# Attention tower with routed experts: down projection joined in one tail, groups of 384 rows for 512

## The reference

```python
# x: (128, 375, 512); q, k, v are its three parts of 125 rows
weight = softmax(einsum('bct,bcs->bts', q * scale, k * scale))
h = einsum('bts,bcs->bct', weight, v)
...
h = h + attn(layernorm(h))          # 8 query heads, 2 key/value heads, softcap 50
x = layernorm(h)
scores = softmax(x @ gate_w)
_, sel = top_k(scores + expert_bias, 2)
...
routed_in = xf[token_idx] * top_scores_sorted[:, None]     # sorted by expert
u = silu(ragged_dot(routed_in, w1, counts)) * ragged_dot(routed_in, w3, counts)
routed_out = ragged_dot(u, w2, counts)
out = silu(xf @ sw1) * (xf @ sw3) @ sw2                    # the shared expert
out = out.at[token_idx].add(routed_out)
h = h + out
```

## Time and profile before

| | us |
|---|---|
| three runs, median | 6056.9 |
| three runs, lowest and highest | 6055.64 and 6059.46 |
| the profiled execution | 6056.73 |
| its span, first to last instruction | 6054.8 |
| TensorE busy | 5857.1 (97%) |
| VectorE busy | 4222.9 (70%) |
| ScalarE busy | 2834.4 (47%) |
| GpSimd busy | 2044.6 (34%) |

### The profile page before, as it was taken

One profiled execution on the slowest core, in us unless ns is written; L12 is line 12 of the kernel. 1 busy time (PEld: TensorE's weight loads), 2 busy tenths in 40 slices (PEclk: granted clock), 3 DMA queues, 4 the chain that ended last, 5 costly groups with the idle time before them and its releaser, 6 DMA issues. The chain is left out here.

```text
span 6054.8 us, 103195 instructions
## 1 busy us (share of the span) xinstructions
PE 5857.1 (97%) x30728; PEld 4825.5 (80%) x30728; DVE 4222.9 (70%) x9884; ACT 2834.4 (47%) x5254; POOL 2044.6 (34%) x1725
## 2 busy tenths in 40 slices
PE   5999999999999999999999999799999999999999
PEld 4888888888888888888888887588888888888887
DVE  4777777777777777777777776566666666666665
ACT  3444444444444444444444443344444444444443
POOL 1333333333333333333333332233333333333332
PEclk8999999999999999999999999899999999999999
DMA  2111111111111111111111111566666666666641
GB/s 71 44 46 47 42 43 47 45 42 44 47 45 42 45 48 43 42 45 48 42 43 47 45 42 31 142 161 162 156 156 156 154 157 157 156 156 160 162 120 50
DMA packets 317085, 504.76 MB, mean 83 GB/s; under 512 B 78645, under 2 KB 151349, under 8 KB 316917
## 3 DMA queue, kind: packets, MB, share of 16 engines
q1 hardware_dynamic: 246132, 372.56, 20.3%
q0 software_dynamic: 70912, 131.71, 11.0%
HBM read 379.30 MB, written 140.28 MB: 86 GB/s over the span
## 5 line engine op out<-in xcount | busy, mean ns | idle before, releaser
L1402 POOL DMA_INDIRECT out_dram<-res,goal x280 | 529.2, 1890 | 1120.1 <-DMA out_dram<-res,goal 688.4
L619 ACT ACTIVATE e<-ps,shift 128x512 f32<-128x512 f32 x512 | 347.4, 683 | 672.4 <-DVE shift L718 635.3
L1146 PE MATMUL ps<-rT_hi,up_hi 128*128 128x512 f32 x1960 | 536.7, 395 | 1.6 <-DVE rT_lo L1310 1.6
L1146 PE MATMUL ps<-rT_lo,up_hi 128*128 128x512 f32 x1960 | 536.9, 395 | 0.0
L1146 PE MATMUL ps<-rT_hi,up_lo 128*128 128x512 f32 x1960 | 536.5, 395 | 0.0
L1146 PEld LDWEIGHTS ps<-rT_hi,up_hi 128*128 128x128 f32 x1960 | 369.1, 188 | 90.0 <-issue 2.0
L1146 PEld LDWEIGHTS ps<-rT_lo,up_hi 128*128 128x128 f32 x1960 | 369.1, 188 | 88.1
L1146 PEld LDWEIGHTS ps<-rT_hi,up_lo 128*128 128x128 f32 x1960 | 368.8, 188 | 88.0
L904 POOL TENSOR_SCALAR ve<-ag 125x1 f32<-125x1 f32 x256 | 57.2, 223 | 1125.2 <-DVE ag L734 1086.2
L1238 ACT ACTIVATE uT_hi<-egb 128x512 fp32r<-128x512 f32 (+1 forms) x280 | 177.1, 632 | 540.7 <-DVE egb L1329 540.5
L1233 ACT ACTIVATE eth<-ps 128x512 f32<-128x512 f32 (+1 forms) x280 | 165.5, 591 | 514.7 <-PE ps L1146 514.4
(11 more groups left out here) (210 smaller groups left out, 15235.1 us busy)
## 6 DMA issues: line engine op xcount, KB each, us to landing
raw<-in_L_ffn_w SPq DMA_DIRECT2D x140, 768.0 KB, 5.2
X<-in_x SPq DMA_DIRECT2D x128, 750.0 KB
raw<-in_L_ffn_w SPq DMA_DIRECT2D x70, 896.0 KB, 4.8
normed_rows<-y SPq DMA_DIRECT2D x128, 250.0 KB
out_dram<-h SPq DMA_DIRECT2D x128, 250.0 KB
raw<-in_L_ffn_w SPq DMA_DIRECT2D x210, 128.0 KB, 6.3
rows<-normed_rows,entries POOLq DMA_INDIRECT x280, 3.9
out_dram<-res,goal POOLq DMA_INDIRECT x280
```

The source lines that it names most:

```text
L619: nc.scalar.activation(e[:, i, :], ps[:, (i + 1) % 2, :], ACT.Exp, scale=QS, bias=shift[:, i:i + 1], accum_out=total[:, i:i + 1]).then_inc ...
L1146: ins = nc.tensor.matmul(ps[:, bank, :], w[a][:, k, col:col + P], rT[b][:, k, :], start=(k == 0 and i == 0), stop=(k == KC - 1 and i == 2))
L1402: nc.gpsimd.indirect_dma_start(out, bass.IndirectOffsetOnAxis(ap=goal[group[1] % 2][:, i:i + 1], axis=0), res[i][:], None, bounds_check=la ...
```

## The change

Three things. First, the shared expert's hidden columns are cut into three blocks of 128 and a tail of 64. The tail stands twice over the partitions, the hidden value's high part on 0 to 63 and its low part on 64 to 127, against the weights' high part on both halves, and again against the weights' low part with zeros below. That makes eleven matmuls of twelve. Second, pieces are moved in the step: four of the down projection now stand ahead of scores 2 and none between scores 2 and 3; ScalarE makes xT high ahead of vT high; GpSimd makes vT low behind the second root and the two scatter DMAs. Third, `GROUP_TILES` is 3, so groups have 384 rows and `NG` is 91. The hidden columns keep their four blocks (three of 128 and the tail), now counted by `BLOCKS` since the tiles are three, and the bank rules for three tiles are written as `LAST_IN_BANK`. The plan divides by three with a multiplication. The loop over groups is two written out, a loop of two, three written out.

```diff
-GROUP_TILES = 4
+GROUP_TILES = 3
...
-                        return nc.tensor.matmul(ps[0:C, 6, :], hT[c][0:HW, k, 0:C], w2s[part][0:HW, k, 0:D],
+                        return nc.tensor.matmul(ps[0:C, 6, :], hT[c][:, k, 0:C], w2s[part][:, k, 0:D],
                                                 start=(k == 0 and part == 0 and c == 0), stop=last)
...
                     if has(3):
-                        down_part(3, 0)
                         down_part(0, 1)
+                        down_part(1, 1)
...
                         last.then_inc(vT_ps.sem, 1)
+                    if has(3):
+                        down_part(2, 1)
+                        pe.wait_ge(hT_lo.sem, hT_lo.at(g))
+                        down_part(0, 0, c=1)
                     if has(0):
                         scores(2)
-                    if has(3):
-                        for k in range(1, HC):
-                            down_part(k, 1)
                     if has(0):
                         scores(3)
...
-                        pe.wait_ge(hT_lo.sem, hT_lo.at(g))
-                        for k in range(HC):
-                            last = down_part(k, 0, c=1, last=(k == HC - 1))
-                        last.then_inc(dn_ps.sem, 1)
+                        for k in (1, 2):
+                            down_part(k, 0, c=1)
+                        down_part(3, 0)
+                        down_part(3, 1, last=True).then_inc(dn_ps.sem, 1)
...
+                    if has(1):
+                        act.wait_ge(xT_ps.sem, xT_ps.at(a))
+                        act.wait_ge(kv_ps.sem, kv_ps.at(f))
+                        hi_part(xT, 3, P).then_inc(xT_hi.sem, 1)
+                    if has(0):
                         act.wait_ge(vT_sb.sem, vT_sb.at(t))
                         act.wait_ge(o_ps.sem, o_ps.at(a))
                         nc.scalar.activation(vT[0][:, :, :], vT_full[:, :, :], ACT.Copy).then_inc(vT_hi.sem, 1)
-                    if has(1):
-                        act.wait_ge(xT_ps.sem, xT_ps.at(a))
-                        act.wait_ge(kv_ps.sem, kv_ps.at(f))
-                        hi_part(xT, 3, P).then_inc(xT_hi.sem, 1)
...
-                        lo_part(hT, 4, HW).then_inc(hT_lo.sem, 1)
+                        nc.vector.tensor_tensor(hT[1][:, 0:3, 0:C],
+                                                ps[:, 4, 0:3 * C].rearrange("p (k c) -> p k c", k=3),
+                                                hT[0][:, 0:3, 0:C].bitcast(F32), ALU.subtract)
+                        nc.vector.tensor_tensor(hT[0][TAIL:P, 3, 0:C], ps[0:TAIL, 4, 3 * C:4 * C],
+                                                hT[0][0:TAIL, 3, 0:C].bitcast(F32),
+                                                ALU.subtract).then_inc(hT_lo.sem, 1)
...
+            LAST_IN_BANK = (1, 3, 2)
...
-                                ins = nc.tensor.matmul(ps[:, bank, :], w[a][:, k, col:col + P], rT[b][:, k, :],
+                                ins = nc.tensor.matmul(ps[:, bank, 0:GROUP], w[a][:, k, col:col + P], rT[b][:, k, :],
                                                        start=(k == 0 and i == 0), stop=(k == KC - 1 and i == 2))
...
-                        pe.wait_ge(res_sb.sem, res_sb.at(back(t, 2)))
+                        pe.wait_ge(res_sb.sem, res_sb.at(back(t, LAST_IN_BANK[i])))
...
                             turn_rows(after, 2)
-                            turn_rows(after, 3)
-                        for i in (2, 3):
-                            down_full(group, i)
-                            down_tail(group, i)
+                        down_full(group, 2)
+                        down_tail(group, 2)
```

More of the change, by code:

```diff
@@ L126, in audio_tower @@
         w3s = resident("w3s", [P, KC, HID])
[L127 removed]
+        w2s = resident("w2s", [P, HC, D])
+        TAIL = HID - 3 * P
+        assert 2 * TAIL == P and HC == 4
         cos_t = sbuf("cos_t", [P, HD], F32, tower)
@@ L181, in _ @@
                     load(raw_3[:, :, :], sw3.rearrange("(k p) h -> p k h", p=P))
-                    load(raw_2[:, :, :], sw2.rearrange("(k p) h -> p k h", p=HW))
+                    load(raw_2[:, 0:3, :], sw2[0:3 * P, :].rearrange("(k p) h -> p k h", p=P))
+                    for q in range(2):
+                        load(raw_2[q * TAIL:(q + 1) * TAIL, 3, :], sw2[3 * P:HID, :])
                     load(cos_t[0:C, :], cos)
@@ L944, in step @@
                                 oob_is_err=False).then_inc(scattered.of(g), 16)
+                    if has(0):
+                        pool.wait_ge(vT_hi.sem, vT_hi.at(t))
+                        pool.wait_ge(o_ps.sem, o_ps.at(a))
+                        alone(pool)
+                        nc.gpsimd.tensor_tensor(out=vT[1][:, :, 0:C], in0=vT_full[:, :, :],
+                                                in1=vT[0][:, :, 0:C].bitcast(F32),
+                                                op=ALU.subtract).then_inc(vT_lo.sem, 1)
                     if has(1):
@@ L1022, in audio_tower @@
             TAIL = HID - FULL * P
-            assert 2 * TAIL == P and T == FULL + 1
+            BLOCKS = FULL + 1
+            assert 2 * TAIL == P and T == 3
+            LAST_IN_BANK = (1, 3, 2)
             HALF = HID + TAIL
             raws = (sbuf("raw1", [P, KC, HID], F32, c2), sbuf("raw3", [P, KC, HID], F32, c2),
-                    sbuf("raw2", [P, T, D], F32, c2))
+                    sbuf("raw2", [P, BLOCKS, D], F32, c2))
             W13 = [[sbuf(f"up_{part}{p}", [P, KC, 2 * HID], F32R, c2) for part in ("hi", "lo")] for p in range(2)]
-            W2 = [[sbuf(f"down_{part}{p}", [P, T, D], F32R, c2) for part in ("hi", "lo")] for p in range(2)]
+            W2 = [[sbuf(f"down_{part}{p}", [P, BLOCKS, D], F32R, c2) for part in ("hi", "lo")] for p in range(2)]
             entries = pair("entries", [P, T, ENTRY])
@@ L1060, in tile_of, with block_of @@
                 return (T * j, T * off + i)
+            def block_of(group, c):
+                j, off = group
+                return (BLOCKS * j, BLOCKS * off + c)
             def landed(group):
@@ L1069, in each_group @@
                 work((0, 1), False, 2)
-                with eng.Fori(1, NG // 2 - 1) as j:
+                with eng.Fori(1, (NG - 3) // 2) as j:
                     work((j, 0), False, 2)
                     work((j, 1), False, 2)
+                work((0, NG - 3), False, 2)
                 work((0, NG - 2), False, 1)
@@ L1372, in work @@
                             rows_lo(after, 2)
-                            rows_lo(after, 3)
                         result(group, 2)
-                        result(group, 3)
                         if left:
@@ L1424, in work @@
                             gather(second, 2)
-                            gather(second, 3)
                         if not left:
```

86 lines of the change are left out of this document (49 added, 37 removed).

## The result

| | before | after |
|---|---|---|
| median, us | 6056.3 (6055.1 to 6059.5, 4 runs) | 5948.4 (5946.1 to 5949.8, 4 runs) |
| ratio | 1 | 0.982, interval 0.980 to 0.984 |
| span of the profiled execution, us | 6054.8 | 5947.1 |

A forecast was written before the change was run, and what follows sets the result against it. TensorE was taken to bound both the attention and expert stages. From 6056.7 us, 74 off the attention stage and 33 off the expert stage gave 5950 us; range 5922 to 6000.

The forecast's parts named there:

- stage one: Attention stage, run per batch: 0.59 us off each of 125 batches, 74 us in all.
- first fill: Start of the expert stage's group pipeline: with drain and added plan operations within 2 us, taken as 0.
- stage two: Expert stage, run per group: 91 groups of 23.91 us against 70 of 31.55, 33 us off.
- Part 1 and 2: Attention stage: one down matmul fewer (0.233 us), others moved ahead of the scores 2 wait; together 0.59 us a batch.
- rival (a): Attention stage gives only the removed matmul, as the scores 2 wait closes later or y or xT stay late: 5995 us; chance 0.12.
- the lower bound of 29 us: Attention stage: least gain expected, from the removed down matmul alone, 0.233 us a batch.
- y can move by the same 0.6: Attention stage, VectorE: with vT low behind GpSimd's root, y comes 0.6 us earlier, and the normalising of e with it.
- Part 3: Expert stage, groups of 384: cheaper up matmuls, fewer down matmuls and transposes, 0.15 us bank wait; group 23.91 us, 33 us off.
- (b): Expert stage gives nothing, because an extra 0.36 us a group is enough: 5983 us; chance 0.13.
- (c): Expert stage: the chain of adds into the output becomes the bound, group 28.5 us, kernel 6368 us; chance 0.04.
- (d): Expert stage: weight traffic or the load-and-matmul pair doesn't shrink with columns, about 6260 us; chance 0.01.

## Why the prediction was right

**The total** is off by only 2 us because stage one and the first fill gave 11 us more (80.8 + 4.0 against 74) and stage two 10 less (22.9 against 33). That the two errors cancel is luck; the mechanism of each part was right.

**Part 1 and 2.** The chain up to scores 2 is fixed, as assumed: the run with the old order of TensorE shows it, and shows that the removed matmul, even with the two new orders beside it, is worth 0.01 to 0.03 us, not the 0.233 that rival (a) and the lower bound of 29 us gave it. It was removed ahead of a wait, so only a longer wait came of it. Nor did the whole change need it much: with 0.19 us of the wait left, a twelfth matmul of 0.233 ahead of scores 2 would cost some 0.04 us a batch, 5 us, an estimate that no run tests. From there the sum holds to the hundredth: 0.59 us between scores 2 and the query projection, projection 0.13 after xT high (forecast 0.14), wait at scores 2 about 0.2. What the sum lacked is a small term behind it. The last 256-column matmuls start at 2008.40 and the transposes of e at 2008.88: 0.48 us, which is the four matmuls' own 4 x 0.120. Before, the same step took 0.56 (2025.34 to 2025.90), because VectorE had e normalised only at 2025.85. The projection now starts 1.46 us after the transposes of xn, not 1.36, and y 3.29 us after them, not 3.44, so e is ready in time. 0.59 and at most 0.08 make the 0.65 a batch, 81 us. The swaps on ScalarE and GpSimd were rightly counted as conditions for the gain: without one 0.44 of it goes, without the other all of it and more. That "y can move by the same 0.6" was true only because of the swap on GpSimd; its price beside ScalarE's new order, 0.94 us, is the largest in stage one, and the forecast didn't work it out, nor that the two swaps hang together. Both expectations for the swaps were off by their size (74 against 58, 88 against 120).

**Part 3.** The interpolated matmul was 0.1755 and is 0.1761: 0.05 a group. The term that was mis-sized is the wait ahead of tile 2's down projection, taken as 0.15 and worth 0.24 by the run with the free bank. The copy, its place and its 0.69 us were right. The working had found 0.17 and rounded it down, and it gave the four transposes 0.39, half of a set of eight, where with the bank free they take 0.36; that is the 0.20 of the trace. The 0.05 of the matmuls and 0.09 of the wait make 0.14, and the group is 0.10 longer than forecast (24.01 for 23.91); the 0.04 between isn't traced. 91 x 0.10 = 9 us, which is the gap between 33 and 23 to 24.

**First fill**, taken as 0, gave 4.0 us: from the last down matmul of stage one to the first up matmul it is 45.4 us instead of 49.4. Three tiles are gathered and turned ahead of the first group, not four; I take that as the cause.

**The rivals.** (a) and (b) are out by the batch and group lengths. (c) is out in this kernel: the add of tile 0 waits for VectorE's copy, and TensorE waits for no add. Whether it comes near at 256 rows is open. (d) is out: 384 columns take 0.176 us, 0.76 of what 512 take. The rule of the Trainium skill ("TensorE: Matmul & The Clock Gate", section "Back-to-back issue gap") that speaks of 131 ns for weight load and matmul at N=512 is not met by any row here: 512 columns with a load for each matmul take 233 ns.

## What to carry to other kernels

Ahead of a wait on a fixed chain a removed instruction is worth next to nothing here (0.01 to 0.03 us of 0.233), and a moved-in one costs nothing while the wait is longer than it. The gain is made behind the wait, and only as far as the next engine's results come earlier too, so look at every queue behind it for a short piece that can let them pass, and at what that piece itself waits for. When a tile is made smaller, the matmul's columns go down in price almost in proportion, but count what stays per group (weight splits, adds that wait for each other) and the double use of a bank: 512 to 384 rows gained 27 us, 384 to 256 lost 250. A buffer that is reused one step sooner costs its wait each time: 0.24 us a group here, and nothing with another bank.

## What the runs showed of the hardware

With a weight load for each matmul, 384 columns take 0.176 us, close to a line with 0.120 for 256, 0.2025 for 448 and 0.233 for 512, although each load itself is shown with 188 ns (line, operation, count, busy us and mean ns of one, from the page):

```profile
L1189 PEld LDWEIGHTS ps<-rT_hi,up_hi 128*128 128x128 f32 x2548 | 457.8, 188 | 9.9 <-issue 2.0
```

The load row is 93% busy in the expert stage (1669 of 1800 us) and yet no wait but the 0.20 us for the bank is put down at a load: the records of loads of 188 ns overlap with each other at one matmul in 120 or 176 ns.

Where an add into the output by GpSimd waited for the landing of the add before, the starts lie 6.05 us apart in the change (DMA share 0.71) and 9.70 in the kernel with 256 rows (0.75). But the kernel before has both, 6.27 and 9.64, at a share of 0.61. So the share of the DMA engines alone doesn't set the length; in these rows the long stretches follow an add whose own issue took 2.9 to 3.0 us and the short ones an add with 1.6, and why is open.

TensorE's granted clock was 1.00 in the kernel with 256 rows, where it stood still for 1.6 to 1.7 us in each group; in the run with the late copies it fell to 0.50 after a standstill of 2.83 us.
